# W1's and W2's blocks loaded by GpSimd's queue instead of the sync engine's, in a one-core two-layer graph network kernel

## The reference

```python
h = relu(layernorm(x));  x = x + L @ (h @ W + b)         # L = scaled (adj + I)
h = relu(layernorm(x))
xw = h @ W1.T                                            # 512 -> 1024
h = layernorm(relu(Dn * (H @ (Be * (H.T @ xw))) + b1)) * gamma + beta
x = x + Dn * (H @ (Be * (H.T @ (h @ W2.T)))) + b2        # 1024 -> 512
```

## Time and profile before

| | |
|---|---|
| median of 3 runs | 1985.3 us (1983.23 to 1985.93) |
| the profiled execution, own time | 1986.17 us |
| its span in the profile | 1984.4 us |
| PE busy | 1961.7 us, 99% |
| DVE busy | 1727.7 us, 87% |
| POOL busy | 1249.4 us, 63% |
| ACT busy | 1083.7 us, 55% |
| SP's DMA queue | 182.55 MB in 467920 packets |

### The profile page before, as it was taken

How to read it: one execution, slowest core, us unless ns; L and a number is a source line. 1 busy time by engine, 2 the same in 40 slices (tenths; PEclk the granted TensorE clock), 3 DMA queues, 4 the chain that set the end, 5 groups by cost and what they waited for, 6 DMA issues and landing times.

```text
span 1984.4 us, 41182 instructions
## 1 busy us (share of the span) xinstructions
PE 1961.7 (99%) x10438; PEld 953.7 (48%) x10438; DVE 1727.7 (87%) x4516; ACT 1083.7 (55%) x2083; POOL 1249.4 (63%) x1934
## 2 busy tenths in 40 slices
PE   7999999999999999999999999999999999999998
PEld 3444444444444444444444444444444444444443
DVE  7988888888888888888888988889888898888985
ACT  6655555555555555555555555555555555555543
POOL 4566666666666666666666666666666666666563
PEclk9999999999999999999999999999999999999999
DMA  6344445444544444444444444444444444544432
GB/s 183 79 95 96 87 90 99 91 88 96 98 87 90 98 91 87 94 101 87 89 93 96 88 90 102 88 88 95 98 87 90 99 91 87 93 101 87 85 82 67
DMA packets 468152, 185.17 MB, mean 93 GB/s; under 512 B 416336, under 2 KB 432720, under 8 KB 467920
## 3 DMA queue, kind: packets, MB, share of 16 engines
q1 hardware_dynamic: 467920, 182.55, 44.9%
HBM read 48.24 MB, written 33.55 MB: 41 GB/s over the span
## 4 chain that ended last, share of the span: by engine, by line
PE 98%; DMA 1%; issue 0%; DVE 0%; ACT 0%; SPq 0%; POOL 0%; DVEq 0%; ACTq 0%; POOLq 0%
PE ps_u L403 34%; PE ps_c L403 33%; PE ps_e L403 16%; PE ps_c L390 1%; PE ps_c L392 1%; PE ps_c L391 1%; PE ps_e L445 1%; PE ps_y L445 1%; PE ps_e L446 1%; PE ps_e L447 1%; PE ps_y L447 1%; PE ps_y L446 1%; PE ps_a L480 1%; PE ps_p L488 0%; PE ps_p L489 0%
## 5 line engine op out<-in xcount | busy, mean ns | idle before, releaser
L599 ACT ACTIVATE h<-z 128x512 f32<-128x512 f32 x256 | 160.8, 629 | 540.2 <-DVE z L792 540.2
L1188 POOL TENSOR_TENSOR rd<-u,neg_half 128x2 f32<-128x2 f32 x128 | 180.9, 1413 | 248.9 <-DVE y L1009 224.5
L403 PE MATMUL ps_c<-w1h,t1h 128*128 128x512 f16 x1024 | 263.7, 380 | 0.9 <-DVE t1l L953 0.9
L403 PE MATMUL ps_c<-w1l,t1h 128*128 128x512 f16 x1024 | 262.9, 379 | 0.0
L403 PE MATMUL ps_c<-w1h,t1l 128*128 128x512 f16 x1024 | 262.8, 379 | 0.0
L403 PE MATMUL ps_u<-w2h,hnT_hi 128*128 128x512 f16 x1024 | 243.2, 380 | 0.0
L403 PE MATMUL ps_u<-w2l,hnT_hi 128*128 128x512 f16 x1024 | 242.3, 379 | 0.0
L403 PE MATMUL ps_u<-w2h,hnT_lo 128*128 128x512 f16 x1024 | 241.9, 379 | 0.0
L1234 POOL TENSOR_TENSOR scr<-x1b,xh 128x512 f32<-128x512 f32 x128 | 229.2, 1791 | 0.3
L1169 POOL TENSOR_TENSOR base<-scr,vq 128x512 f32<-128x512 f32 x128 | 223.4, 1745 | 7.9 <-ACT vq L593 4.4
L792 DVE SCALAR_TENSOR_TENSOR z<-ps_c,dn,b_all 128x512 f32<-128x512 f32 x256 | 191.0, 746 | 29.4 <-PE ps_c L403 29.2
(11 more groups left out here) (124 smaller groups left out, 4431.5 us busy)
## 6 DMA issues: line engine op xcount, KB each, us to landing
x_t<-in_x_dram SPq DMA_DIRECT2D x128, 256.0 KB, 2.9
out_dram<-out_t SPq DMA_DIRECT2D x128, 256.0 KB, 2.3
adj_t<-in_adj_dram SPq DMA_DIRECT2D x128, 64.0 KB, 2.6
raw_w<-in_W1T_dram SPq DMA_DIRECT2D x4, 512.0 KB, 8.4
h0T_hi<-h_hi SPq DMA_TRANSPOSE x128, 2.4
h0T_lo<-h_lo SPq DMA_TRANSPOSE x128, 2.5
raw_w<-in_W2T_dram SPq DMA_DIRECT2D x8, 256.0 KB, 4.9
hnT_hi<-hn_hi SPq DMA_TRANSPOSE x128, 3.1
```

The lines of the kernel that those rows point to most:

```text
L403: mm = pe.matmul(ps, t[:, j * 128:(j + 1) * 128], w[:, j, cols], start=(n == 0 and j == 0), stop=(n == 2 and j == blocks - 1))
L599: act.activation(h[:, cols], z[:, cols], ACT.Relu).then_inc(s_h[n], 1)
L1188: pool.tensor_tensor(rd0[:, m, :], u0[:, m, :], neg_half[:, :], ALU.pow).then_inc(s_pp0, 1)
```

## The change

The sync engine's queue no longer issues W1's four and W2's eight blocks; its other transfers keep their order and close up. GpSimd's queue gets a `load_weight` of its own. Before each of its four groups it waits until W's last block has landed; each block adds to the same semaphore as before, so all who read the blocks are unchanged. The groups are W1 blocks 0 and 1 behind `do_bias0(0)`, W1 blocks 2 and 3 behind `weight_power(0)`, W2 blocks 0 to 3 behind `scale_bias`, and W2 blocks 4 to 7 behind `weight_power(1)`. W2's blocks now come in the order of their numbers (before: 0, 1, 3, 2, 6, 7, 4, 5).

```diff
@@ sync engine
             load_x(1)
-            load_weight(1, raw_w1, W1T, range(0, 4))
             load_gamma_beta()
             do_tr0h(0); do_tr0l(0)
-            load_weight(2, raw_w2, W2T, range(0, 2))
             load_x(2)
             load_x(3)
-            load_weight(2, raw_w2, W2T, range(3, 4))
-            load_weight(2, raw_w2, W2T, range(2, 3))
             load_adj(3)
-            load_weight(2, raw_w2, W2T, range(6, 8))
-            load_weight(2, raw_w2, W2T, range(4, 6))
             load_row(b2_all, b2, s_rows)
@@ gpsimd
+            def load_weight(n, dst, src, blocks):
+
+                pool.wait_ge(s_raw_w[0][KI - 1], 16)
+                for j in blocks:
+                    pool.dma_start(dst[:, j, :], src[j * 128:(j + 1) * 128, :]).then_inc(s_raw_w[n][j], 16)
+
@@ gpsimd
             do_rd0(0); do_bias0(0)
+            load_weight(1, raw_w1, W1T, range(0, 2))
             weight_power(0)
+            load_weight(1, raw_w1, W1T, range(2, 4))
             do_rd0(1); do_bias0(1)
             scale_bias()
+            load_weight(2, raw_w2, W2T, range(0, 4))
             weight_power(1)
+            load_weight(2, raw_w2, W2T, range(4, 8))
             do_cx(0); do_rd0(2); do_u1(0); do_sc1(0); do_dn1(0); do_nm1(0); do_bias0(2); do_x1b(0); do_qdn(0)
```

## The result

The changed kernel takes 1988.88 us in the median of 20 runs (1987.73 to 1990.42), the kernel before 1985.49 us (1983.09 to 1986.61, 20 runs). The ratio is 1.002, with a 95% interval of 1.0014 to 1.0026: 2.8 to 5.2 us slower, some 3.4 us. The forecast was 2.2 us slower, 1987.5 us, in a range of 1984.3 to 1992.5 us. The profiled execution took 1987.73 us with a span of 1985.9 us.

What follows compares the result with a forecast made beforehand. PE's work bounds the kernel from 52.16 us on, waits for others bound the start. With 1.0 us per GpSimd issue, later W2 landings put y(0) 2.2 us late: 1985.3 + 2.2 = 1987.5 us, range 1984.3 to 1992.5.

Steps and rivals of the forecast that it cites:

- Only the start counts: Whole kernel: PE is full from 52.16 us on, so time changes only by as much as that moment moves.
- Step 1: Sync engine's queue without W1 and W2: x(2) issued 1.1 us earlier, b perhaps earlier; counted at nothing, at most 0.5 us.
- Step 2: GpSimd's line in the start: each DMA issue costs 1.0 us, with 0.43 us as low end and 2.32 us from above.
- rival A: GpSimd from 13.5 us to W1's scale: issues stretched while DVE works delay the power for W1; +5 to +7.5 us, chance 0.20.
- Step 3: GpSimd's line at 1.0 us an issue: scale_bias ends at 18.4, W2's blocks land later, y(0) starts 2.2 us late.
- the landing: W2's first blocks in the start: 256 KB lands 3.57 us after issue, block 0 at 22.0 us, block 1 at 23.0.
- cover of 1.2 us: PE's Y0(0) after W1's last block: would end at 26.0 us, still ahead of y(0) at 27.26.
- Covered steps: Start: added waits for W cost nothing; W1's last block, W1's magnitude and do_cx(0) at 27.4 us stay hidden.
- Rival B: Loads in the start land faster than 3.0 us after short issues, so no cost: 1984.8 to 1985.8 us, chance 0.12.
- Rival C: PE's clock: another drop in the pause before Z0(0) gives 1989.6 us, a spared drop at 50 us 1985.4; chance 0.08.

## Why the prediction was right, and which terms were not

The sign, the place and the range held: 3.4 us slower, nothing gained, and all of it made before 30 us. Point by point:

- **Only the start counts.** Right. Behind Z0(2) and up to 1900 us PE is full in both, apart from the 0.47 us at 66.56 us and the clock. The prediction's rows stop at 1900 us; behind that PE idles another 7.8 us in the kernel before and 7.7 in the changed one, which its "from 52.16 us on" passes over. It makes no difference here, since it is the same in both.
- **Step 1, gains at nothing.** Right. b did land earlier (the power for W at 12.24 instead of 12.91 us, and W's scale 0.8 us earlier), and that went into ACT's wait for W2. x(2) was issued 1.8 us earlier (15.43 instead of 17.22) but landed 0.4 us later (21.97 instead of 21.56), so of that gain nothing came.
- **Step 2, an issue at 1.0 us.** Too high. It costs 0.55 to 0.67 us, near the low end of 0.43. The 0.4 us more than on the sync engine that the prediction gave beside it is a difference of times to the first byte, not of the time an issue takes on GpSimd's line; that was some 0.1 us (0.54 against 0.43). With the low cost rival A is gone: DVE was at work beside eight of the twelve issues, and none took more than 0.79 us, which is what the first one on its queue takes in all runs but two. In these two, with W2 alone on GpSimd, the first issue did run into a VectorE copy (17.71 us, 0.69 us long), and took 0.99 us. The Trainium skill, "SBUF — State Buffer", section "SBUF: two separate sides", gives 3.1 us for such a DMA under a VectorE copy and 0.62 us alone. These runs have 0.2 us more at the issue; that the copy was the reason isn't shown, and a wait of the size that the page gives isn't there. (By the prediction's own steps, with eight issues ahead of the power for W1, the cost beyond 1.0 us grows by 8 us for each us, and +4 us would be reached at 1.4 us per issue, not 1.3.)
- **Step 3, POOL's line.** Its sum for scale_bias was 18.4 us; it ended at 17.1. The power for W1 behind the issues (22.4 us) was the wrong wait: it came at 23.64 us because W1's last block was late. The run with all eight issues ahead of it shows that the line had room for four more.
- **The term that was mis-sized: the landing.** I took 3.0 us from issue to landing, the median of W's blocks at the empty start, plus 0.57. The same view of the kernel before has W1 and W2 themselves, and in the median they took longer (W2's block 0 alone landed in 3.0 us there):

```profile
raw_w<-in_W1T_dram SPq DMA_DIRECT2D x4, 512.0 KB, 8.4
raw_w<-in_W2T_dram SPq DMA_DIRECT2D x8, 256.0 KB, 4.9
```

  Measured from each block's turn in the issues, W2's block 0 took 6.7 us (17.09 to 23.83) and W1's last 7.5 (13.3 to 20.82), where 3.6 to 4.2 were in the sum. By the low issue cost the sum had given +0.8 us at y(0); with the landings as they were it is +4.2. The two errors had opposite signs; that the forecast of 2.2 us lay so near is in part luck.
- **What I left out.** The forecast named W1's issues as moved from 5.43 to 10.2 us, and still costed only the last block's landing. It didn't ask what the DMA engines do meanwhile. They stood idle for 3 us, in a start in which their busy share was 0.91, so all behind moves back. The run with W1 held on one queue gives this a price by itself: 2.45 us at W1's last block for some 2.4 us of idle DMA engines, and 1.9 us at y(0). The cover of 1.2 us that I gave to W1's last block was gone.
- **Covered steps.** The four waits for W cost nothing, as said. So did do_cx(0), at 26.81 us.
- **Rival B** was half present: the issues were short, but the landings weren't. **Rival C**, the clock, cost nothing extra; it favoured the changed kernel in the profiled pair. A drop ahead of Z0(0), as it feared, did come where W2 stood alone on GpSimd (0.50 from 26 to 29 us).

Accounted for at y(0), by one trace each: the late moment of W1, 1.9 us; GpSimd's queue with its spread issues at that moment, another 1.8 us; W2's two groups on top, 0.5 us, which is no more than the scatter of the marks. The medians show a loss for each of the three kernels (held, W1 alone, changed: +3.1, +4.1 and +3.4 us) but can't confirm the split. W2's groups alone would cost 5.5 us, of which 2.2 are the rows b2 and b1 that move ahead of them; beside the late W1 most of it is hidden, since ACT then waits for both. What remains open is why W1, from its first issue at about 11 us, takes 9.7 to 10.3 us on GpSimd's queue (six runs) and 8.4 on the sync engine's (one run). The last of its issues comes 2.45 us behind the first there against 1.3 us, and from its own issue the last block lands in 7.2 to 7.8 us against 7.0, so most of the difference is of the size of the spread; but the run that brought the four issues together made W1 later and not earlier. For W1 the transposes are ruled out. For W2 they, x(2) and the later transfers together stretch the landing in the changed kernel; how much of the 5.5 us for its block 0 in the run with the rows away is theirs wasn't tried.

The Trainium skill, "DMA: Bandwidth & Descriptors", section "Issuing engines are not separate DMA queues", says that DMAs of all engines run on the same 16 DMA engines, and that a second issuing engine saves only issue time. The runs agree. W2's blocks on GpSimd's queue landed in 4.2 to 4.6 us with the sync engine's transfers away and in 6.7 to 9.0 us beside them, and the run with W1 on GpSimd at 7.61 us, 0.3 us from the kernel before, shows that the queue brings nothing by itself.

## What to carry to other kernels

When loads move to another engine's queue, cost first the moment at which they are issued, and ask what the DMA engines do until then: a stretch without outstanding transfers, in a start that waits for them, is paid (here 2.45 us at the last block for 2.4 us of idle, and 1.9 us at the mark that counts). A landing time belongs to its surroundings more than to its size (a block of W2: 3.0, 4.2 or 8.0 us); take it from a transfer with the same load ahead of it, and look at what the old queue now brings forward. For a change of a few microseconds in two milliseconds, compare a mark inside the trace as well as the ends, because the clock alone can move the end by 3 us.

## What the runs showed of the hardware

- A DMA issue occupied GpSimd for 0.53 to 0.62 us, 256 KB or 512 KB alike, and the first one on its queue for 0.79 us (0.99 us in the two runs where it began 0.2 us ahead of a VectorE copy of 128x1024 f32). On the sync engine's queue W2's issues took 0.42 to 0.57 us in the kernel before, W1's 0.43 to 0.96 us.
- Between the first issue on GpSimd (10.89 us) and the first traffic there were 1.1 us or more; the engines moved nothing from 11 to 12 us and 82 GB/s from 12 to 13. With the sync engine's first issue of W1 at 10.71 us they moved 61 GB/s from 11 to 12 us, and W1's first block landed 3.65 us after its issue, against 4.1 to 4.3 us on GpSimd's queue at that moment. The changed kernel:

```profile
11.00:12.00 1.00, 0.00 (x0) 0.00 (x0) 0.97 (x4) 1.00 (x2) 0.99 (x2) 1.00 0.00 0
12.00:13.00 1.00, 0.00 (x0) 0.00 (x0) 0.51 (x6) 0.19 (x1) 0.98 (x3) 1.00 0.64 82
```

- From Z0(2) to the span's end the 14 profiled executions took 1931.0 to 1933.8 us; the five at 1933.3 or more (the kernel before and four others) had a slower first matmul in Z0(2), 0.45 to 0.58 us; it took 0.38 us in the rows of the changed kernel. In four of these five the last graph's eight matmuls took 2.95 to 3.19 us as well, where the changed kernel has 1.90. So they did in two others (3.12 and 3.15 us), which took 1932.8 and 1932.7 us from Z0(2) to the end.
